# Weight column and destinations of the routed tiles: from GpSimd to VectorE

## The chip, the core and the metric

One core of a Trainium2 chip runs the kernel. The metric is the device time of one execution in microseconds. Before the change it is 798.48 us, the median of three runs (797.54, 798.48, 799.52).

## What is computed

One transformer block with adaptive layer norm on x of shape 4 x 1024 x 128: causal attention with 16 heads of 8, then a mixture of experts. Only the second half matters here:

```python
shared_out = expert(x, sg, su, sd)          # silu(x g^T) * (x u^T), times d
logits = x @ wr.T + rb                      # 7 experts
scores, idx = top_k(softmax(logits), 2)
scores = scores / scores.sum(-1)
out = shared_out
for e in range(7):
    out = out + w[..., e] * expert(x, rg[e], ru[e], rd[e])
x = x + gb * out                            # hidden width 352, model width 128
```

The kernel computes a routed expert only for the tokens that chose it.

## The kernel before

Attention fills the first 500 us or so; the change doesn't touch it. Then the 4096 tokens are normalised, the shared expert is computed in eight chunks of 512 tokens, and the router's choices are turned into slots. This is done in two groups of 2048 tokens. Each token has two choices, so a group has 4096 rows to place, and with the filling up of each expert's last tile 38 tiles of 128 rows (`STG`), 76 in all (`ST`).

A row that is scattered has 142 numbers (`RW`): 128 of the modulated token, 7 weights, one for each expert, and 7 numbers from which the destination of the result follows, one for each expert. GpSimd scatters the rows to the tensor `slot_rows_scratch` in DRAM with indirect DMAs of 128 rows (`scatter`, L782), 32 for each group. The last 24 of the second group are issued between the first routed tiles (`scatter_second`).

Each engine has its own instruction stream, and semaphores join them. The routed stage is a software pipeline written out as one function `slot_step(i, r)` for each engine. `tile(i, r, lag)` gives the tile that step r works on at that lag: tile r - lag. In step r:

- SP loads the rows of tile r+5 into `srow` (L638, four buffers). It waits until the transpose of tile t-4 (`s_rowT`) and the destinations of tile t-4 (`s_meta`) are done.
- TensorE transposes the rows of tile r+1 (L1831), multiplies tile r by gate and up (L1843), tile r-2 by down (L1854), and transposes the hidden values of tile r-1 (L1864). The transpose of tile t waits for `h_lo` of tile t-1.
- ScalarE copies the high part `h_hi` of tile r+1 (L1080), forms silu of tile r (L1087), scales the result of tile r-2 by the weight column into `y_s` (L1096, four buffers, so it waits until the scatter of tile t-4 has landed), and copies `hidT` of tile r-1 (L1103, L1105).
- VectorE forms `h_lo` of tile r+1 (L1525) and the hidden product `hid_s` of tile r (L1532). In the last twelve steps it combines the results of the first group as well (`combine`, L1510 to L1515).
- GpSimd, for tile r+2, waits for the rows, loads the tile's expert number from `expert` into a register (L831), copies that expert's weight column into `s_weight` (L832) and adds that expert's destination column to the tile's spare slots into `s_dest` (L835), a ring of twelve. Then it scatters `y_s` of tile r-3 to `routed_results_scratch` (L844), and up to step 21 it issues one scatter of the second group (L782).

`slot_steps` unrolls the steps for PE, ACT and DVE. GpSimd's and SP's middle steps are loops on the engine. The streams of VectorE and ScalarE start at step -1, that of GpSimd at step -2.

When all scatters of a group have landed, SP reads the results back (`read_results`); VectorE alone, for the second group with GpSimd (L861), adds them up and SP stores the output.

The destinations are integers held in the bits of float columns: L1388 writes them as int32, and the constant `spare` holds int32 bits (L1903).

Of the kernel before, what the change touches and what calls it, by code (L numbers as in the profile page):

```python
# [20 lines left out]
I32 = mybir.dt.int32  # L21
F32R = mybir.dt.float32r
ALU = mybir.AluOpType
# [3 lines left out]
B, S, D = 4, 1024, 128  # L27
# [4 lines left out]
T = 128  # L32
# [10 lines left out]
NE, NI = 7, 352  # L43
# [14 lines left out]
GRP = 2  # L58
# [5 lines left out]
ST = GRP * STG  # L64
RW = D + 2 * NE
SB = 4
SU = 3 * SB

CST, _at = {}, 0
# [137 lines left out]
def adaln_block(nc, x_d, wq_d, wk_d, wv_d, wo_d, sw_g_d, sw_u_d, sw_d_d, wr_d, rb_d, c_d, wmod_d,  # L207
# [10 lines left out]
    with ctx:  # L218
        def sb(name, shape, dt=F32, at=None):
            return (at or ctx).enter_context(nc.sbuf_tensor(name, shape, dt))  # L220

        def sem(name):
            return ctx.enter_context(nc.semaphore(name))
# [9 lines left out]
        cst = sb("cst", [128, CSTW])  # L233
# [68 lines left out]
        rows = sb("rows", [T, NT, RW], at=moe)  # L302
# [13 lines left out]
        tot = sb("tot", [T, GT, NE], at=moe)  # L316
# [7 lines left out]
        expert = sb("expert", [1, ST], I32, at=moe)  # L324
# [4 lines left out]
        srow = sb("srow", [T, SB, RW], at=moe)  # L329
        s_weight = sb("s_weight", [T, ST], at=moe)  # L330
        s_dest = sb("s_dest", [T, SU], I32, at=moe)
# [120 lines left out]
        s_expert = sem("s_expert")  # L452
# [3 lines left out]
        s_srow = [sem(f"s_srow{j}") for j in range(SB)]  # L456
        s_rowT = sem("s_rowT")
        s_meta = sem("s_meta")
# [10 lines left out]
        s_y_out = [sem(f"s_y_out{j}") for j in range(SB)]  # L469
# [32 lines left out]
        def slot_steps(eng, first, last, body):  # L502

            for s in range(first, last + 1):
                body(0, s)

        def tile(i, r, lag):

            t = SU * i + (r - lag)
            if isinstance(t, int) and not 0 <= t < ST:
                return None
            return t, (r - lag) % SB, SU // SB * i + (r - lag) // SB
# [5 lines left out]
        GTILES = [slice(g * GT, (g + 1) * GT) for g in range(GRP)]  # L520
# [4 lines left out]
        def needs(eng, semaphore, value):  # L525

            if not (isinstance(value, int) and value <= 0):
                eng.wait_ge(semaphore, value)
# [149 lines left out]
        def _(pool):  # L678
# [123 lines left out]
            for x in range(TOP * GT):  # L802
                k, t = divmod(x, GT)
# [16 lines left out]
            for n in range(ahead):  # L820
                scatter_second(n)

            pool.wait_ge(s_expert, GRP)

            def slot_step(i, r):
                at = tile(i, r, -2)
                if at:

                    t, j, times = at
                    pool.wait_ge(s_srow[j], 16 * times + 16)  # L830
                    e = pool.value_load(expert[0:1, bass.ds(t, 1)], min_val=0, max_val=NE - 1)  # L831
                    nc.gpsimd.tensor_copy(s_weight[:, bass.ds(t, 1)], srow[:, j, bass.ds(D + e, 1)])  # L832
                    d = (r + 2) % SU
                    needs(pool, s_y_out[j], 16 * (times - SU // SB + 1))
                    nc.gpsimd.tensor_tensor(s_dest[:, d:d + 1], srow[:, j, bass.ds(D + NE + e, 1)].bitcast(I32),  # L835
                                            cst[:, bass.ds(CST["spare"][0] + t, 1)].bitcast(I32), ALU.add).then_inc(s_meta, 1)
                at = tile(i, r, 3)
                if at:
                    t, j, times = at
                    pool.wait_ge(s_meta, t + 1)  # L840
                    pool.wait_ge(s_y, t + 1)
                    pool.sem_inc(s_seen_pool, 1)
                    d = (r - 3) % SU
                    nc.gpsimd.indirect_dma_start(y_d, bass.IndirectOffsetOnAxis(ap=s_dest[:, d:d + 1], axis=0),  # L844
                                                 y_s[:, j, :], None).then_inc(s_y_out[j], 16)
# [264 lines left out]
        def _(dve):  # L1110
            chain = [0]

            def link(ins):

                chain[0] += 1
                ins.then_inc(s_link, 1)
                dve.wait_ge(s_link, chain[0])

            V = nc.vector
# [102 lines left out]
            def ring_item(x):  # L1222

                _, kind, n, h, what = RING_PIECES[x]
                m, bank = n % 3, ring_bank(x)
                if kind in BY_ACT:
# [156 lines left out]
            def slots(g, incl):  # L1383
                before = ps[:, GROUPED, 0:GT * NE].rearrange("p (t e) -> p t e", t=GT)
                link(V.tensor_tensor(tot[:], incl, tot[:], ALU.subtract))
                link(V.tensor_tensor(tot[:], tot[:], before, ALU.add))
                link(V.tensor_tensor(tot[:], tot[:], tbase[:].unsqueeze(1).to_broadcast((T, GT, NE)), ALU.add))
                link(V.tensor_tensor(rows[:, GTILES[g], D + NE:RW].bitcast(I32), rows[:, GTILES[g], D + NE:RW], tot[:], ALU.subtract))  # L1388
                for k in range(TOP):
                    link(V.tensor_scalar(pick[:], rank[:], float(k), None, ALU.is_equal))  # L1390
                    link(V.tensor_tensor(chosen[:], pick[:], tot[:], ALU.mult))
                    link(V.reduce_sum(slot_f[:, k, :], chosen[:], AX.X))
                    V.tensor_copy(slot[:, k, GTILES[g]], slot_f[:, k, :]).then_inc(s_slot, 1)  # L1393
# [112 lines left out]
            def combine(n, part):  # L1506
                ts = chunk(n)
                if part == 0:
                    dve.wait_ge(s_y_in[n], 16 * TOP)
                    link(V.tensor_tensor(acc[:, n % 2, :, :], y_in[0][:, ts, :], y_in[1][:, ts, :], ALU.add))  # L1510
                elif part == 1:
                    link(V.tensor_tensor(acc[:, n % 2, :, :], acc[:, n % 2, :, :],
                                         gate_b[:, n * CG // TB:n * CG // TB + 1, :].to_broadcast((T, CG, D)), ALU.mult))
                else:
                    V.tensor_tensor(xs[:, ts, :], xs[:, ts, :], acc[:, n % 2, :, :], ALU.add).then_inc(s_res, 1)  # L1515
# [3 lines left out]
            def slot_step(i, r):  # L1519
                at = tile(i, r, -1)  # L1520
                if at:
                    t, j, _ = at
                    t2 = j % 2
                    dve.wait_ge(s_h_hi, t + 1)
                    V.tensor_tensor(h_lo[:, t2, :], ps[:, 0, 0:T], h_hi[:, t2, :].bitcast(F32), ALU.subtract).then_inc(s_h_lo, 1)  # L1525
                at = tile(i, r, 0)
                if at:
                    t, j, _ = at
                    t2 = j % 2
                    dve.wait_ge(s_ssilu, t + 1)  # L1530
                    needs(dve, s_shidT, t - 1)
                    V.tensor_tensor(hid_s[:, t2, :], sg[:, t2, :], ps[:, 2 + 2 * t2, 0:NI], ALU.mult).then_inc(s_shid, 1)  # L1532
                if isinstance(i, int) and first_combine <= r < first_combine + 3 * GC:
                    combine(*divmod(r - first_combine, 3))
            slot_steps(dve, -1, ST + 1, slot_step)


            for n in range(GC, NC):
# [389 lines left out]
```

## Time and profile before

| | |
|---|---|
| runs | 797.54, 798.48, 799.52 us |
| profiled execution | 797.6 us, its span 795.9 us |
| TensorE busy | 686.8 us, 86% |
| VectorE busy | 573.4 us, 72% |
| ScalarE busy | 545.9 us, 69% |
| GpSimd busy | 342.0 us, 43% |

The times of an execution count a little more than its span, which goes from the first to the last instruction. A row of a time line has the start in us from the span's start, the duration, the engine (PE is TensorE, PEld its weight load, DVE VectorE, ACT ScalarE, POOL GpSimd; a q behind it is the engine's sequencer), the line, the operation and, in brackets, how long the engine was idle before and what ended that. "issue" means that the engine waited for nothing that the profile shows. Busy time over the whole span mixes stages that have different limits, so the stretches of the routed stage are to be read one by one.

### The profile page before, as it was taken

The numbers are of one execution on the slowest core, as the hardware profiler recorded it, in microseconds if no ns is written. First come the engines' busy times: TensorE is split into PE (matmuls) and PEld (weight loads), VectorE is DVE, ScalarE is ACT, GpSimd is POOL, SyncE is SP. The second block draws the span as 40 slices with busy tenths as digits, with TensorE's granted clock in tenths as the row PEclk, the third lists the DMA queues.
The fourth block names the chain that finished last, engine by engine and source line by source line (L and its number), as shares of the span: only waits on it lengthen the run. The fifth ranks groups of instructions, "written<-read, shape, count | busy, mean of one in ns | idle before, by whom it ended". The sixth has DMA issues, their size and how long they took to land.

```text
span 795.9 us, 18082 instructions
## 1 busy us (share of the span) xinstructions
PE 686.8 (86%) x5304; PEld 395.3 (50%) x5304; DVE 573.4 (72%) x2042; ACT 545.9 (69%) x1013; POOL 342.0 (43%) x551
## 2 busy tenths in 40 slices
PE   2986899999999999999999986678869989999970
PEld 1553123333333333333333434567659889999960
DVE  5797889999999999999999834574773323333543
ACT  2785259889989888989888788544325556666640
POOL 1367613232322322232322123235657887666652
PEclk9999569999999999999999999699999999999995
DMA  9246021111111111111110079202233322223425
GB/s 260 83 156 219 1 74 47 39 30 29 47 47 48 47 28 30 41 46 47 48 37 14 1 136 178 68 23 81 63 92 78 82 76 81 66 68 104 131 87 158
DMA packets 64760, 59.46 MB, mean 75 GB/s; under 512 B 10798, under 2 KB 52398, under 8 KB 64668
## 3 DMA queue, kind: packets, MB, share of 16 engines
q1 hardware_dynamic: 58924, 46.85, 23.3%
q0 software_dynamic: 4480, 9.64, 3.4%
q10 hardware_dynamic: 1264, 1.84, 0.7%
q8 instruction: 46, 0.75, 0.4%
q14 instruction: 46, 0.38, 0.2%
HBM read 33.57 MB, written 24.33 MB: 73 GB/s over the span
## 4 chain that ended last, share of the span: by engine, by line
PE 59%; DVE 18%; ACT 9%; issue 7%; DMA 3%; POOL 1%; SPq 1%; ACTq 1%; DVEq 0%; POOLq 0%
PE ps L1658 13%; PE ps L1602 10%; PE ps L1843 9%; PE ps L1681 7%; PE ps L1854 6%; DVE junk L1238 5%; ACT probs L973 5%; PE ps L1864 3%; PE ps L1758 2%; PE ps L1636 2%; DVE junk L1210 2%; PE ps L1750 2%; DMA routed_results_scratch<-y_s,s_dest 1%; PE ps L1831 1%; DVE rot L1193 1%
## 5 line engine op out<-in xcount | busy, mean ns | idle before, releaser
L973 ACT ACTIVATE probs<-ps 128x1024 f32<-128x1024 f32 (+1 forms) x320 | 285.5, 941 | 34.5 <-PE ps L1681 32.1
L1210 DVE CUSTOM_DVE_ANT_0 junk<-ps,tri 128x512 f32<-128x512 f32 (+3 forms) x512 | 218.5, 487 | 13.9 <-PE ps L1602 11.6
L1602 PE MATMUL ps<-ka,qa 61*128 61x256 bf16 (+3 forms) x788 | 186.7, 325 | 10.0 <-DVE rowmax L1210 3.0
L775 POOL TENSOR_SCALAR_AFFINE_SELECT probs<-probs 128x512 f32<-128x512 f32 x128 | 79.7, 634 | 191.8 <-ACT probs L973 191.8
L1658 PE MATMUL ps<-probs,v 128*32 128x512 f32 (+3 forms) x1536 | 157.7, 498 | 1.3 <-POOL probs L775 1.1
L1681 PE MATMUL ps<-qa,ka 64*128 64x512 bf16 (+3 forms) x768 | 144.6, 331 | 7.7 <-ACT probs L973 5.6
L1602 PEld LDWEIGHTS ps<-ka,qa 61*128 61x128 bf16 x788 | 53.0, 95 | 159.8 <-DVE rowmax L1210 80.4
L844 POOL DMA_INDIRECT routed_results_scratch<-y_s,s_dest x76 | 76.2, 1003 | 41.0 <-issue 35.0
L782 POOL DMA_INDIRECT slot_rows_scratch<-rows,slot x64 | 64.1, 1001 | 56.6 <-DVE slot L1393 30.1
L1243 DVE TENSOR_REDUCE leftmax<-ps 128x1 f32<-128x512 f32 x120 | 78.4, 686 | 8.5 <-PE ps L1602 8.5
L1532 DVE TENSOR_TENSOR hid_s<-sg,ps 128x352 f32<-128x352 f32 x76 | 39.6, 521 | 46.2 <-ACT sg L1087 46.0
L1854 PE MATMUL ps<-wd,hidT 128*128 (+1 forms) x456 | 64.3, 277 | 5.8 <-ACT hidT L1105 5.8
L1525 DVE TENSOR_TENSOR h_lo<-ps,h_hi 128x128 fp32r<-128x128 f32 x76 | 22.2, 291 | 59.7 <-ACT h_hi L1080 59.3
L1854 PEld LDWEIGHTS ps<-wd,hidT 128*128 128x128 f32 (+1 forms) x456 | 60.6, 192 | 7.4 <-issue 7.3
L1658 PEld LDWEIGHTS ps<-probs,v 128*32 128x32 f32 x1536 | 33.8, 108 | 54.5 <-issue 49.3
L1681 PEld LDWEIGHTS ps<-qa,ka 64*128 64x128 bf16 x768 | 42.5, 94 | 33.4 <-ACT probs L973 21.2
L1087 ACT ACTIVATE sg<-ps 128x352 f32<-128x352 f32 x76 | 35.2, 463 | 33.8 <-PE ps L1843 32.0
L1096 ACT ACTIVATE y_s<-ps,s_weight 128x128 f32<-128x128 f32 x76 | 27.9, 367 | 33.5 <-PE ps L1854 25.4
L1238 DVE CUSTOM_DVE_ANT_0 junk<-ps,above 128x256 f32<-128x256 f32 x136 | 49.3, 419 | 0.0
L749 POOL TENSOR_TENSOR mrest<-mneg,mparts 32x128 f32<-32x128 f32 x16 | 6.7, 417 | 92.7 <-ACT mparts L936 92.7
L1843 PE MATMUL ps<-w_hi,h_hi 128*128 x152 | 45.3, 380 | 1.2 <-issue 1.1
L1210 DVE DVE_READ_ACCUMULATOR2_ANT rowmax<- 128x1 f32 x512 | 42.6, 83 | 0.1
(195 smaller groups left out, 1168.4 us busy)
## 6 DMA issues: line engine op xcount, KB each, us to landing
slot_rows_scratch<-cst SPq DMA_DIRECT2D x1, 5396.0 KB, 36.1
srow<-slot_rows_scratch SPq DMA_DIRECT2D x76, 71.0 KB
k_parts_scratch<-qk_parts SPq DMA_DIRECT2D x12, 320.0 KB, 2.7
ka<-k_parts_scratch SPq DMA_DIRECT2D x32, 120.0 KB
q_parts_scratch<-qk_parts SPq DMA_DIRECT2D x12, 256.0 KB, 2.6
qa<-q_parts_scratch SPq DMA_DIRECT2D x32, 96.0 KB
ka<-k_parts_scratch SPq DMA_DIRECT2D x32, 80.0 KB
xs<-in_x SPq DMA_DIRECT2D x4, 512.0 KB, 9.4
```

What stands on the lines that cost most here:

```text
L775: nc.gpsimd.affine_select(out=p, in_=p, compare_op=ALU.is_ge, fill=0.0, base=0, pattern=[[0, HQ], [1, T]], channel_multiplier=-1).then_inc ...
L782: nc.gpsimd.indirect_dma_start(slot_d, bass.IndirectOffsetOnAxis(ap=slot[:, k, t:t + 1], axis=0), rows[:, t, :], None).then_inc(s_scatter[ ...
L844: nc.gpsimd.indirect_dma_start(y_d, bass.IndirectOffsetOnAxis(ap=s_dest[:, d:d + 1], axis=0), y_s[:, j, :], None).then_inc(s_y_out[j], 16)
L973: nc.scalar.activation(probs[(n * NS + s) % 4][:, 2 * h:2 * h + 2, 0:UNTIL[s] - FROM[s]], ps[:, 2 * h:2 * h + 2, FROM[s]:UNTIL[s]], ACT.Ex ...
L1210: last = V.tensor_tensor_reduce(out=junk[:, bank - 5, at:at + w], in0=ps[:, bank, at:at + w], in1=tri[:, CH - w:CH], scale=1.0, scalar=LOW ...
L1238: last = V.tensor_tensor_reduce(out=junk[:, bank - 5, cols], in0=ps[:, bank, cols], in1=above[:, h, q - CG, :], scale=1.0, scalar=LOW, op0 ...
L1243: last = V.reduce_max(leftmax[m][:, row, q - CG:q - CG + 1], ps[:, bank, :], AX.X)
L1602: last = MM(ps[:, bank, at:at + w], qa[m][g0:g0 + KS, c0 + q * T:c0 + (q + 1) * T], ka[m][g0:g0 + KS, d0 + k0:d0 + k0 + w], start=True, st ...
L1658: last = MM(ps[VW * h:VW * (h + 1), 4, q0:CH], v4[m][:, k, h, :], probs[(n * NS + s) % 4][:, h, p0:p0 + CH - q0], start=begins, stop=ends ...
L1681: last = MM(ps[:, 2 * pair + g, at:at + CH - q0], ka[m][g * HG:(g + 1) * HG, pair * KW + kb * T:pair * KW + (kb + 1) * T], qa[m][g * HG:(g ...
L1843: last = MM(ps[:, 1 + 2 * t2 + g, 0:NI], ht[:, t2, :], wt[:, bass.ds(e, 1), g, :], start=(k == 0), stop=(k == 2))
L1854: last = MM(ps[:, 6, 0:D], hidT[0:w, t2, c, :], wd[0:w, bass.ds(e, 1), c, :], start=(c == 0), stop=(c == len(IC) - 1))
```

## The change

The two operations of L832 and L835, with their waits and the load of the expert number, go from GpSimd's `slot_step` to VectorE's. There they stand behind `hid_s` and ahead of the combining, for the same tile r+2 in step r. VectorE's steps now start at -2, behind a wait for `s_expert`. The destinations are kept as floats; the sum converts to int32 when it writes `s_dest`.

```diff
@@ GpSimd
-            pool.wait_ge(s_expert, GRP)
-
             def slot_step(i, r):
-                at = tile(i, r, -2)
-                if at:
-
-                    t, j, times = at
-                    pool.wait_ge(s_srow[j], 16 * times + 16)
-                    e = pool.value_load(expert[0:1, bass.ds(t, 1)], min_val=0, max_val=NE - 1)
-                    nc.gpsimd.tensor_copy(s_weight[:, bass.ds(t, 1)], srow[:, j, bass.ds(D + e, 1)])
-                    d = (r + 2) % SU
-                    needs(pool, s_y_out[j], 16 * (times - SU // SB + 1))
-                    nc.gpsimd.tensor_tensor(s_dest[:, d:d + 1], srow[:, j, bass.ds(D + NE + e, 1)].bitcast(I32),
-                                            cst[:, bass.ds(CST["spare"][0] + t, 1)].bitcast(I32), ALU.add).then_inc(s_meta, 1)
                 at = tile(i, r, 3)
@@ VectorE, slots()
-                link(V.tensor_tensor(rows[:, GTILES[g], D + NE:RW].bitcast(I32), rows[:, GTILES[g], D + NE:RW], tot[:], ALU.subtract))
+                link(V.tensor_tensor(rows[:, GTILES[g], D + NE:RW], rows[:, GTILES[g], D + NE:RW], tot[:], ALU.subtract))
@@ VectorE, slot_step()
                     V.tensor_tensor(hid_s[:, t2, :], sg[:, t2, :], ps[:, 2 + 2 * t2, 0:NI], ALU.mult).then_inc(s_shid, 1)
+                at = tile(i, r, -2)
+                if at:
+                    t, j, times = at
+                    dve.wait_ge(s_srow[j], 16 * times + 16)
+                    e = dve.value_load(expert[0:1, bass.ds(t, 1)], min_val=0, max_val=NE - 1)
+                    V.tensor_copy(s_weight[:, bass.ds(t, 1)], srow[:, j, bass.ds(D + e, 1)])
+                    d = (r + 2) % SU
+                    needs(dve, s_y_out[j], 16 * (times - SU // SB + 1))
+                    V.tensor_tensor(s_dest[:, d:d + 1], srow[:, j, bass.ds(D + NE + e, 1)],
+                                    cst[:, bass.ds(CST["spare"][0] + t, 1)], ALU.add).then_inc(s_meta, 1)
                 if isinstance(i, int) and first_combine <= r < first_combine + 3 * GC:
                     combine(*divmod(r - first_combine, 3))
-            slot_steps(dve, -1, ST + 1, slot_step)
+            dve.wait_ge(s_expert, GRP)
+            slot_steps(dve, -2, ST + 1, slot_step)
@@ constants
-           "spare": (np.arange(T)[:, None] + T * np.arange(ST)[None, :]).astype(np.int32).view(np.float32)}
+           "spare": np.arange(T)[:, None] + T * np.arange(ST)[None, :]}
```

## Rows read from the trace of the kernel before

**Rows 1.** Stretches: from:to, length, busy PE PEld DVE ACT POOL, clock, DMA, GB/s.
```profile
603.00:632.00 29.00, 28.93 (x218) 28.28 (x217) 11.09 (x27) 18.63 (x66) 23.01 (x40) 1.00 0.29 78
632.00:643.00 11.00, 8.34 (x48) 7.49 (x47) 2.44 (x6) 4.49 (x17) 9.15 (x16) 0.84 0.30 79
...
661.00:731.00 70.00, 70.00 (x524) 68.16 (x523) 26.53 (x65) 46.54 (x163) 45.76 (x105) 1.00 0.24 69
```
**Rows 2.** Time line of ScalarE, y_s of tiles 0, 12, 14, 21 and 23.
```profile
603.28 0.37 ACT L1096 ACTIVATE y_s<-ps,s_weight 128x128 f32<-128x128 f32 x1 [0.31 <-PE ps L1854]
...
629.05 0.37 ACT L1096 ACTIVATE y_s<-ps,s_weight 128x128 f32<-128x128 f32 x1 [0.31 <-PE ps L1854]
...
636.73 0.37 ACT L1096 ACTIVATE y_s<-ps,s_weight 128x128 f32<-128x128 f32 x1 [3.55 <-DMA routed_results_scratch<-y_s,s_dest]
...
655.37 0.37 ACT L1096 ACTIVATE y_s<-ps,s_weight 128x128 f32<-128x128 f32 x1 [2.52 <-DMA routed_results_scratch<-y_s,s_dest]
...
659.70 0.37 ACT L1096 ACTIVATE y_s<-ps,s_weight 128x128 f32<-128x128 f32 x1 [0.31 <-PE ps L1854]
```
**Rows 3.** Time line of GpSimd: first scatter of a result, one turn, scatter of tile 19.
```profile
604.45 1.00 POOL L844 DMA_INDIRECT routed_results_scratch<-y_s,s_dest  x1 [1.62 <-issue]
...
612.75 1.00 POOL L844 DMA_INDIRECT routed_results_scratch<-y_s,s_dest  x1 [0.16 <-issue]
614.06 0.97 POOL L782 DMA_INDIRECT slot_rows_scratch<-rows,slot  x1 [0.30 <-issue]
615.03 0.19 POOL L832 COPY s_weight<-srow 128x1 f32 x1
...
615.52 1.00 POOL L844 DMA_INDIRECT routed_results_scratch<-y_s,s_dest  x1 [0.16 <-issue]
...
657.04 1.00 POOL L844 DMA_INDIRECT routed_results_scratch<-y_s,s_dest  x1 [0.16 <-issue]
```
**Rows 4.** Chain of work that ended last: start us, us, what.
```profile
632.14 4.41 DMA routed_results_scratch<-y_s,s_dest
...
651.51 3.68 DMA routed_results_scratch<-y_s,s_dest
```
**Rows 5.** Time line of GpSimd, a scatter that y_s released.
```profile
708.15 1.00 POOL L844 DMA_INDIRECT routed_results_scratch<-y_s,s_dest  x1 [0.79 <-ACT y_s L1096]
```
**Rows 6.** Time line of VectorE and TensorE, a turn in the steady stretch.
```profile
712.22 0.29 DVE L1525 TENSOR_TENSOR h_lo<-ps,h_hi 128x128 fp32r<-128x128 f32 x1 [0.75 <-ACT h_hi L1080]
...
713.03 0.52 DVE L1532 TENSOR_TENSOR hid_s<-sg,ps 128x352 f32<-128x352 f32 x1 [0.51 <-ACT sg L1087]
...
713.33 0.27 PE L1831 MATMUL ps<-eye,srow 128*128 128x128 f32 x1
...
714.30 0.29 DVE L1525 TENSOR_TENSOR h_lo<-ps,h_hi 128x128 fp32r<-128x128 f32 x1 [0.75 <-ACT h_hi L1080]
```
**Rows 7.** Scatters and short VectorE operations; GpSimd's sequencer by line (ns min/median/max).
```profile
575.64 1.36 POOL L782 DMA_INDIRECT slot_rows_scratch<-rows,slot  x1 [0.56 <-DVE hid L1416]
577.32 0.96 POOL L782 DMA_INDIRECT slot_rows_scratch<-rows,slot  x1 [0.31 <-issue]
...
577.38 0.18 DVE L1359 COPY scan<-scan 128x28 f32<-128x28 f32 x1
...
579.51 0.15 DVE L1373 COPY tend<-tend 128x1 f32<-128x1 f32 x1
...
L831 POOLq FUSED_REGOPS  x112: 52/152/176, 591.9 to 760.8; - x112
L831 POOLq TENSOR_LOAD <-expert x76: 284/289/511, 591.4 to 760.5; - x76
```
**Rows 8.** Time line of VectorE, a step with combining.
```profile
755.40 0.68 DVE L1512 TENSOR_TENSOR acc<-acc,gate_b 128x512 f32<-128x512 f32 x1
756.30 0.29 DVE L1525 TENSOR_TENSOR h_lo<-ps,h_hi 128x128 fp32r<-128x128 f32 x1 [0.22 <-ACT h_hi L1080]
```
**Rows 9.** Waits of SP's queue: in total us, times, longest.
```profile
SPq L528 <- POOL s_dest L835: 63.5, 37, 4.9
```

## The prediction

> **What bounds the kernel now.** I read the busy time by stretch first, to see which engine is full where [rows 1]. The routed tiles run from about 595 to 774 us of the span, one tile a turn, 76 in all. From 661 to 731 TensorE is busy 70.00 of 70.00 us at full granted clock: its own work is the bound, and in that stretch VectorE is busy 26.53 us and GpSimd 45.76. From 603 to 632 it is the same (28.93 of 29.00). From 632 to 643 it is not: TensorE has 8.34 of 11.00 us and the granted clock has a mean of 0.84. So something else ends turns there, and the change can only pay in such a place.
>
> The time line of ScalarE says what [rows 2]. y_s of tile 0 starts at 603.28, of tile 12 at 629.05: 2.147 us a tile, TensorE's pace. Then come two long waits, 3.55 us ahead of tile 14 and 2.52 ahead of tile 21, both ended by a landing of the scatter to routed_results_scratch: y_s has four buffers, so tile t waits for the scatter of tile t-4. At TensorE's pace tile 23 would start at 603.28 + 23 x 2.147 = 652.66; it starts at 659.70. The stage has lost 7.0 us, and nothing after it gives them back, since TensorE has no idle time behind 661.
>
> Why do the scatters land late? GpSimd's time line in the early half [rows 3]: scatter of a tile at 612.75, second-group scatter at 614.06, the weight copy at 615.03, the sum behind it, next scatter of a tile at 615.52. This is 2.77 us a turn against 2.147 for TensorE. Nineteen such turns lie between the scatter of tile 0 (604.45) and that of tile 19 (657.04): 52.59 / 19 = 2.768. GpSimd falls behind by 0.62 us a turn until the four buffers are used up; from tile 13 on it sets the pace. Behind tile 19 there are no more second-group scatters and it catches up.
>
> **GpSimd's turn, after the change.** Two instructions leave it, with the load of the expert's number and its register arithmetic. From the copy's start (615.03) to the next scatter (615.52) there are 0.49 us [rows 3]. In their place comes the gap that this engine shows between one indirect DMA and the next, 0.30 us (the idle time ahead of the one at 614.06, same rows). A turn is 2.77 - 0.49 + 0.30 = 2.58 us, 0.19 less, and 19 turns give 3.6 us. The scatter of tile 19 would start at 604.45 + 19 x 2.58 = 653.5 instead of 657.04. The first one doesn't move: it waits for y_s of tile 0 anyway.
>
> How much of 3.6 reaches the end hangs on the landings. From the start of a scatter to the y_s that waits for it there were 4.59 us at tile 10 (632.14 to 636.73) and 3.86 at tile 17 (651.51 to 655.37) [rows 2, 4]; at tile 19 no more than 2.66 (657.04 to 659.70) [rows 2, 3]. If tile 17's landing is as slow again, y_s of tile 21 starts at 604.45 + 17 x 2.58 + 3.86 = 652.2, which is 3.2 us earlier; with 2.66 at tile 19, tile 23 starts at 653.5 + 2.66 = 656.1, 3.6 us earlier. I take 3.4. A landing of 4.6 at tile 19 would leave 1.6. Still GpSimd-bound in either case: tile 23 would be 3.5 us behind TensorE's pace, not 7.
>
> Upper end: the gap ahead of a scatter might be the 0.16 that stands behind the sum now [rows 3], not 0.30. Then 0.33 x 19 = 6.3 us, close to the 7.0 that are there at all. Lower end: the gap might be the lead that a scatter shows when it is released by y_s, 0.79 us [rows 5]; that is a rival below. I take 0.30 because it is the gap of a DMA behind a DMA, which the new pattern is, and in this stretch y_s has long been ready.
>
> **GpSimd elsewhere.** From 661 on its turn is already shorter than TensorE's and ends by waiting for y_s; a shorter turn gives only more waiting. Behind the last tile nothing of the changed work is left. Nothing for either.
>
> **VectorE: two instructions and a load more per tile.** Its steady turn [rows 6]: h_lo at 712.22 (0.29), hid_s at 713.03 (0.52), h_lo again at 714.30, so it works 0.81 of 2.15 us, and from hid_s's end (713.55) there are 0.75 us free. The new work stands in that gap. A 128x28 copy on this engine takes 0.18, a 128x1 copy 0.15, and I take the sum of two columns for no more [rows 7]: 0.3 to 0.36 for both. Before them the queue loads the expert's number, 0.29, and computes with it, 0.15 on GpSimd's sequencer [rows 7]; this can run under hid_s, as GpSimd's copy starts right at the end of its scatter. Lower bound 0.3, upper bound all in series 0.36 + 0.29 + 0.15 + as much again for computing the addresses = 0.95. Even then h_lo is 0.2 late, and TensorE asks for it only with the next transpose: h_lo ended at 712.51, that transpose started at 713.33, 0.82 of slack. Cost zero; VectorE could take 1.3 us a turn before it were the bound.
>
> In the last twelve steps VectorE also combines the first group: 0.68 us behind hid_s, and h_lo then follows with 0.22 idle [rows 8]. With 0.3 to 0.36 more h_lo is 0.1 late under 0.8 of slack: zero again. With the load in series too the turn would be 0.81 + 0.68 + 0.95 = 2.44, over 2.15 by 0.29, for nine steps: 2.6 us.
>
> **The waits that move with it.** VectorE now waits for the rows of tile t behind hid_s of t-2. What is queued behind that wait is h_lo of the same tile t, which needs the transpose of those very rows, and the combining, which has slack of its own; so the wait holds nothing back that TensorE asks for. The wait for the landing of tile t-12 is far from binding with four y_s buffers. The loads on SP's queue wait for the destination of tile t-4; SP stood for it 63.5 us in 37 waits [rows 9], since GpSimd ran behind. They will start earlier, and TensorE gains nothing, as it didn't wait for rows in those turns. The float form of the constants and of the 112-element subtraction costs what the integer one does.
>
> **Rivals.** (a) The port. VectorE's copy and GpSimd's descriptor writing may exclude each other. For it: a second-group scatter that ran beside VectorE's large operations took 1.36 us instead of 0.96 [rows 7]. Against it: the next one, with two short copies inside, took 0.96. If each turn's copy costs the scatter its own 0.15 to 0.19 us, the 3.6 us are eaten: 0.0 to 0.8 gained, 798 us.
> The Trainium skill (SBUF — State Buffer, "Who interferes with whom", and the warning box on SWDGE above it) has this as a rule: a float copy from SBUF to SBUF on VectorE can lock GpSimd out of the port pair and starve its descriptors; by it the sum would be about nothing. The second row speaks against it for copies as short as these.
> (b) Slower: the lead of a scatter is exposed. The sequencer of GpSimd now has only one DMA, not a copy and a sum, behind which it can prepare the next scatter with its two waits. If the 0.79 of [rows 5] shows up in each of the 19 turns, the turn is 2.58 + 0.49 = 3.07, 0.3 more than now: 5.7 us slower, 804. It decides from a gap of 0.49 up. Against: the second-group DMA behind a scatter starts after 0.30 already.
> (c) The combining steps all in series: 2.6 of the 3.4 lost, 797.7.
> (d) A larger gain, 5 to 7 us, with the gap of 0.16 or with quick landings: 792.5.
> (e) It doesn't do what it says: the landings, not GpSimd's starts, set the pace; then 0 to 1.5.
>
> **How the numbers follow.** The profiled run took 797.6 us with a span of 795.9; the median of the three is 798.5 (797.5 to 799.5). From the profiled run 797.6 - 3.4 = 794.2; from the median 798.5 - 3.4 = 795.1, which I give. What separates no change from a change here is about 0.3%, 2.4 us. Chances: forecast (gain 2.4 to 4.6) 0.56, (d) 0.08, (a), (c), (e) and slow landings, gain 0 to 2.4, together 0.23, a small loss under 2.4 from the same causes 0.03, (b) or another loss over it 0.10. Faster 0.64, same 0.26, slower 0.10. The range leaves out the far half of (d) and nearly all of (b): 792.5 to 799.
>
> **What would show it.** Right: in GpSimd's early turns a gap of 0.30 between DMAs and 2.58 a turn, the scatter of tile 19 near 653.5, less than 4 us of ScalarE's waits for landings, h_lo still followed by the transpose without a wait, same turns of 2.15 behind 661. Wrong: scatters over 1.00 us long in those turns (a), gaps of 0.5 and more (b), h_lo released by VectorE's own previous instruction and TensorE waiting for it (c). What I trust least is the length of the landings, which I can't derive.

## The result, and the profile after

Both kernels were timed twenty times on one chip. Before: median 799.16 us (797.54 to 800.44). After: 796.96 us (795.37 to 799.25). The ratio is 0.9976, interval [0.9969, 0.9983]: the change takes off 1.4 to 2.5 us. The forecast was 3.4. The profiled execution of the kernel after took 797.11 us; its span is the first line of its page. The times quoted leave out one execution of an experiment and one of the kernel before (825.81 and 917.96 us) that ran at a lower granted clock (0.817 and 0.695) throughout.

```profile
span 795.4 us, 18051 instructions
PE 689.1 (87%) x5304; PEld 395.6 (50%) x5304; DVE 595.4 (75%) x2194; ACT 546.3 (69%) x1013; POOL 313.5 (39%) x398
```

GpSimd is busy 28.5 us less and VectorE 22.0 us more; neither number says what became of the time. The stretches of [rows 1], read in the kernel after (from:to, length, busy PE PEld DVE ACT POOL, clock, DMA, GB/s), with the steps in which VectorE combines as the last row:

```profile
603.00:632.00 29.00, 29.00 (x220) 28.41 (x219) 14.86 (x54) 19.03 (x67) 20.27 (x22) 1.00 0.30 84
632.00:643.00 11.00, 10.82 (x80) 10.22 (x79) 5.33 (x21) 7.01 (x25) 8.51 (x9) 1.00 0.35 97
...
661.00:731.00 70.00, 70.00 (x523) 68.21 (x522) 35.91 (x131) 46.51 (x163) 31.54 (x33) 1.00 0.25 70
745.00:773.00 28.00, 23.91 (x167) 21.71 (x165) 16.93 (x47) 15.11 (x52) 13.41 (x13) 0.95 0.27 80
```

From 632 to 643 TensorE now works 10.82 of 11.00 us, where it had 8.34, and the granted clock is 1.00 instead of 0.84. That is the gain. The last row is where something was lost; the same stretch before:

```profile
745.00:773.00 28.00, 25.42 (x188) 24.16 (x186) 16.04 (x33) 16.95 (x60) 19.61 (x32) 1.00 0.29 88
```

TensorE had 25.42 us busy there and has 23.91, with fewer instructions in the same 28 us, since each turn is longer.

GpSimd's turn, the forecast's main term, answers to [rows 3]: the first scatter of a result, a second-group scatter, the next scatter of a result, and the one of tile 19.

```profile
605.32 0.96 POOL L831 DMA_INDIRECT routed_results_scratch<-y_s,s_dest  x1 [2.94 <-issue]
606.59 0.96 POOL L782 DMA_INDIRECT slot_rows_scratch<-rows,slot  x1 [0.30 <-issue]
607.85 0.96 POOL L831 DMA_INDIRECT routed_results_scratch<-y_s,s_dest  x1 [0.30 <-issue]
...
653.36 0.96 POOL L831 DMA_INDIRECT routed_results_scratch<-y_s,s_dest  x1 [0.31 <-issue]
```

The gap is the 0.30 that was forecast. The turn is (653.36 - 605.32) / 19 = 2.528 us, not 2.58: every scatter takes 0.96 us, where those of a result took 1.00 before.

To see what reaches the end, take as loss of a tile how far its y_s is behind TensorE's pace: (y_s of tile t) - (y_s of tile 0) - 2.1475 x t. In us, from ScalarE's time line:

```
tile                       24     60     64     73     75
before                   6.94   6.95   8.05   7.99   7.72
after                    2.41   2.46   4.17   5.89   6.19
after less before       -4.5   -4.5   -3.9   -2.1   -1.5
```

Five stages can be read from it. By tile 24, 4.5 us are won. Up to tile 60 nothing moves. From 60 to 64, where SP reads the first group's results back ahead of the rows of tile 65, both kernels lose, the one after 0.6 more. From 64 to 73, in the steps with combining, the kernel after loses 1.72 us, the one before gains 0.06: 1.8. In the last two tiles the kernel after falls back by 0.6 more, and that is the clock: the granted clock of this execution falls to 0.83 from 768 to 771 and to 0.50, the level of 1.2 GHz, behind it, with TensorE idle 0.75 us ahead of each of the last two groups of down matmuls; the last group of six then takes 1.50 us, where it took 0.93 before.

```profile
767.76 0.93 PE L1852 MATMUL ps<-wd,hidT 128*128 x6 [0.75 <-ACT hidT L1092]
768.52 0.49 PE L1862 MATMUL ps<-eye,hid_s 128*128 128x128 f32 x3
769.77 1.50 PE L1852 MATMUL ps<-wd,hidT 128*128 x6 [0.75 <-ACT hidT L1092]
```

Before, the same idle stretches stood there at full clock, and in an experiment with the same combining steps (the last one below) the clock stayed at 1.00 up to 773, and in each of the twelve experiments' traces the last two tiles lose nothing. So this 0.6 belongs to the execution.

Tile 0 starts 0.88 us later in the kernel after (604.16 against 603.28), which no median can show. In the experiments below this start lies anywhere from 602.1 to 605.7, also where nothing ahead of the stage differs. Most of the 0.88 stands there long before the changed code runs: GpSimd's last copy of `v` in the attention starts at 436.77 against 436.25, VectorE's last write of `slot` at 585.75 against 584.96. So it too belongs to the execution. What is left is 1.5 us, inside the measured interval.

Where does the turn of the combining steps get longer? VectorE in two of them, against [rows 8]:

```profile
749.99 0.28 DVE L1512 TENSOR_TENSOR h_lo<-ps,h_hi 128x128 fp32r<-128x128 f32 x1
750.40 0.52 DVE L1519 TENSOR_TENSOR hid_s<-sg,ps 128x352 f32<-128x352 f32 x1
751.14 0.15 DVE L1525 COPY s_weight<-srow 128x1 f32 x1 [0.22 <-issue]
751.28 0.16 DVE L1528 TENSOR_TENSOR s_dest<-srow,cst 128x1 int32<-128x1 f32 x1
751.36 0.68 DVE L1497 TENSOR_TENSOR acc<-y_first,y_second 128x512 f32<-128x512 f32 x1
752.08 0.29 DVE L1512 TENSOR_TENSOR h_lo<-ps,h_hi 128x128 fp32r<-128x128 f32 x1
752.97 0.52 DVE L1519 TENSOR_TENSOR hid_s<-sg,ps 128x352 f32<-128x352 f32 x1 [0.61 <-ACT sg L1074]
753.71 0.15 DVE L1525 COPY s_weight<-srow 128x1 f32 x1 [0.22 <-issue]
753.86 0.16 DVE L1528 TENSOR_TENSOR s_dest<-srow,cst 128x1 int32<-128x1 f32 x1
753.93 0.69 DVE L1499 TENSOR_TENSOR acc<-acc,gate_b 128x512 f32<-128x512 f32 x1
754.65 0.29 DVE L1512 TENSOR_TENSOR h_lo<-ps,h_hi 128x128 fp32r<-128x128 f32 x1
```

From hid_s to h_lo VectorE has no idle time but the 0.22 ahead of the copy, and h_lo no longer waits for ScalarE's h_hi (in [rows 8] it did, for 0.22). h_lo starts 0.42 us behind the end of h_hi in the mean of eight such turns (tiles 68 to 75), 0.07 before. TensorE in the first of these turns, from the chain of work that ended last (start us, us, what):

```profile
750.54 0.33 PE ps L1862 x3
750.87 0.11 PE ps L1829
750.98 0.24 issue
751.21 1.23 PE ps L1841 x6
```

Behind the transpose of the rows (L1829) TensorE stands 0.24 us with "issue", waiting for nothing that the profile names, and the gate-up (L1841) follows. h_lo ended at 750.27 (749.99 + 0.28), the gate-up started at 751.21: 0.94 us. TensorE's sequencer in that time (ns min/median/max, first and last start):

```profile
L1820 PEldq TENSOR_LOAD <-expert x1: 298/298/298, 750.4 to 750.4; - x1
L1820 PEldq FUSED_REGOPS  x1: 151/151/151, 750.8 to 750.8; - x1
L1820 PEldq SEQ_ASSERT  x1: 18/18/18, 751.0 to 751.0; - x1
```

It loads the expert's number from 750.4 on, right behind the end of h_lo, and is busy with it to 751.0. This pointed to the cause.

### The profile page after: what moved, and what is told of

Same layout as the page of the kernel before. It is cut to its first block, busy times and chain, and to the rows that moved or that the text cites. A ratio compares the mean times of both kernels' runs of the same rounds, so it can differ in the third digit from the quotient of the medians.

```text
span 795.4 us, 18051 instructions
## 1 busy us (share of the span) xinstructions
PE 689.1 (87%) x5304; PEld 395.6 (50%) x5304; DVE 595.4 (75%) x2194; ACT 546.3 (69%) x1013; POOL 313.5 (39%) x398
## 4 chain that ended last, share of the span: by engine, by line
PE 60%; DVE 17%; ACT 9%; issue 7%; DMA 3%; SPq 1%; POOL 1%; ACTq 1%; DVEq 0%; POOLq 0%
PE ps L1656 13%; PE ps L1600 10%; PE ps L1841 9%; PE ps L1679 7%; PE ps L1852 6%; DVE junk L1225 5%; ACT probs L960 5%; PE ps L1862 3%; PE ps L1756 2%; PE ps L1634 2%; DVE junk L1197 2%; PE ps L1748 2%; DMA routed_results_scratch<-y_s,s_dest 1%; PE ps L1573 1%; PE ps L1829 1%
## 5 line engine op out<-in xcount | busy, mean ns | idle before, releaser
L831 POOL DMA_INDIRECT routed_results_scratch<-y_s,s_dest x76 | 74.6, 981 | 72.5 <-DVE s_dest L1528 51.6
L1841 PE MATMUL ps<-w_hi,h_hi 128*128 x152 | 45.0, 378 | 2.0 <-issue 1.8
L1748 PE MATMUL ps<-h_hi,ws_hi 128*128 128x512 f32 (+1 forms) x48 | 22.0, 459 | 18.7 <-DVE hid L1403 18.7
```

Source lines behind the costliest of these rows:

```text
L1841: last = MM(ps[:, 1 + 2 * t2 + g, 0:NI], ht[:, t2, :], wt[:, bass.ds(e, 1), g, :], start=(k == 0), stop=(k == 2))
```

## The theory and its rival

TensorE's queue in one step is: wait for h_lo of tile t, transpose the rows of tile t+1, load the expert's number of tile t into a register, compute with it, gate-up of tile t. The load stands behind the wait. In the kernel before the least distance from the end of h_lo to the next gate-up is 0.91 us in the 32 turns of the steady stretch, and 0.96 in the mean; after, in the combining steps, 0.91 and 0.97. Only the last tile comes below (0.82 and 0.64): with no rows left to transpose, its wait for h_lo stands behind the load. A least value that recurs, whatever the stretch, looks like a floor and not like slack. Theory B: nothing of the 0.82 that I read in [rows 6] was free; an h_lo that is late makes the next gate-up late. Its rival, the prediction's own account: h_lo has slack, and the loss has another source (the read-back, landings, the port).

## The experiments

Each median stands beside that of the kernel before on the same chip. All losses are those of the table's definition.

**Combining out of the way.** In the kernel after, the twelve combining parts come behind the last routed step:

```diff
-                if isinstance(i, int) and first_combine <= r < first_combine + 3 * GC:
-                    combine(*divmod(r - first_combine, 3))
...
             slot_steps(dve, -2, ST + 1, slot_step)
+            for n in range(GC):
+                for part in range(3):
+                    combine(n, part)
```

On SP's queue the second read-back goes ahead of the first store.

> The changed kernel, but the twelve parts of combining the first group (8.3 us of VectorE) stand behind the last step, where VectorE is idle for 11.8 us, and SP reads back the second group before it stores the first. Theory A: VectorE's chain in the last steps is short again, turns of 2.15, 2.0 to 2.5 us faster than the changed kernel, less up to 1 us for four stores that now stand ahead of the last ones: 794.5 to 796. Rival (the loss isn't VectorE's): 797 or a little more.

Measured: 795.77 against 799.12, ratio 0.9961 [0.9947, 0.9975]. That is in the expected range, but only 1.2 us under the kernel after, and the two intervals overlap. The trace is clearer: the loss is 3.88 at tile 64 and 3.66 at tile 73, so these steps cost nothing. VectorE with the two new instructions but without the combining:

```profile
751.24 0.15 DVE L1525 COPY s_weight<-srow 128x1 f32 x1 [0.22 <-issue]
751.39 0.16 DVE L1528 TENSOR_TENSOR s_dest<-srow,cst 128x1 int32<-128x1 f32 x1
751.78 0.29 DVE L1512 TENSOR_TENSOR h_lo<-ps,h_hi 128x128 fp32r<-128x128 f32 x1 [0.23 <-ACT h_hi L1067]
```

h_lo waits for h_hi again. So the loss of the combining steps needs both: the new work and the combining on one engine.

**The new work back on GpSimd for the tiles whose steps combine** (67 to 75):

```diff
+                if at and isinstance(at[0], int) and at[0] >= LATE:      # LATE = 67, GpSimd's stream
...
+                    nc.gpsimd.tensor_copy(s_weight[:, bass.ds(t, 1)], srow[:, j, bass.ds(D + e, 1)])
...
-                if at:
+                if at and at[0] < LATE:                                  # VectorE's stream
```

> The changed kernel, but for tiles 67 to 75 (those whose weight and destination fall into the steps with combining) GpSimd forms them again, from floats, with one more copy to int32. Theory A: in those steps VectorE's extra 0.5 us stands in the chain hid_s, copy, sum, combining, h_lo, gate-up and stretches the turns from 2.15 to about 2.4. Then this is 2.0 to 2.5 us faster than the changed kernel (797.0), so about 794.7 or a ratio of 0.994 to 0.995 to the kernel before, and turns of 2.15 in the last ten steps. Rival: the time lost at the end comes from the loads of the rows, or what goes missing is a later start of the whole stage from run to run; then it is within 0.5 us of the changed kernel.

Measured: 796.24 against 799.12, 0.9966 [0.9957, 0.9976]. The loss from tile 64 to 73 is 0.20 us, where the kernel after has 1.72: as expected. The time is only 0.7 us better than the 796.96 of the kernel after, and the two intervals overlap; in this profile the read-back cost 3.6 us (2.47 at tile 60, 6.07 at 64). So the trace bears out where the time goes; the 2 us in the median are not shown.

**h_lo late, alone.** The kernel before, with one copy of 128x64 ahead of each h_lo:

```diff
                     dve.wait_ge(s_h_hi, t + 1)
+                    V.tensor_copy(late[:], h_hi[:, t2, 0:64].bitcast(F32))
```

> The kernel before, with one more VectorE copy of 128x128 or less (0.15 to 0.2 us) ahead of h_lo in every step, of a tile nobody reads. The prediction held that h_lo has 0.82 us of slack: then no change. Theory B: gate-up never starts less than 0.91 us behind the end of h_lo, since TensorE's sequencer waits for h_lo before it loads the expert's number (0.30 + 0.15 us) for the next products, and that floor is reached in about every second turn already; the chain spans two tiles. Then each turn gets about half of the delay longer: 0.06 to 0.1 us times 70, 4 to 7 us slower in all, turns of about 2.22 us.

Measured: 800.34 against 799.12, 1.0022 [1.0013, 1.0031]: 1.0 to 2.5 us slower. A turn of VectorE and TensorE's next gate-up:

```profile
715.39 0.19 DVE L1526 COPY late<-h_hi 128x64 f32<-128x64 f32 x1 [0.75 <-ACT h_hi L1081]
715.50 0.28 DVE L1527 TENSOR_TENSOR h_lo<-ps,h_hi 128x128 fp32r<-128x128 f32 x1
```

The copy is overlapped by the subtraction, so h_lo is late by 0.12 us, not by 0.20. The turn goes from 2.147 to 2.192 in the steady stretch, 0.045 for 0.12: some 0.07 us a turn was free, and the rest was paid. The least distance to the gate-up is 0.91 as ever. Against 0.82 of slack the result should have been none. The sign is theory B's; its 4 to 7 us were too much. They took 0.06 to 0.1 us, half of the copy's length, as paid in 70 turns. A turn of the steady stretch pays 0.045, and those that GpSimd paces pay nothing (the loss at tile 24 is 6.68, not above before's 6.94).

**TensorE's load ahead of its wait.** The decisive one, on both kernels:

```diff
             def slot_step(i, r):
+                at = tile(i, r, 0)
+                if at:
+                    expert_of(i, at[0], r)
                 at = tile(i, r, -1)
```

Nothing but the place of a register load, 0.30 us long with 0.15 of arithmetic behind it, in TensorE's stream differs. On the kernel after:

> The changed kernel with one thing moved: TensorE loads the expert's number of tile r at the head of step r, ahead of its wait for h_lo, not behind the transpose. Theory B: the 0.91 us between the end of h_lo and gate-up were that load behind that wait. Then the shortest distance falls to 0.4 to 0.6 us, the turns with combining go from 2.37 back to 2.15 or less though VectorE does what it did, the steady turns may shrink from 2.147 to 2.10, and the kernel is 2 to 4 us faster than the changed one: 793 to 795. Rival: VectorE is busy too long in those steps in itself; then the turns stay at 2.37 and the time at 797.

Measured: 790.65 against 799.03, 0.9871 [0.985, 0.9891]. VectorE and TensorE in the combining steps:

```profile
741.37 0.69 DVE L1497 TENSOR_TENSOR acc<-y_first,y_second 128x512 f32<-128x512 f32 x1
742.09 0.29 DVE L1512 TENSOR_TENSOR h_lo<-ps,h_hi 128x128 fp32r<-128x128 f32 x1
...
742.52 0.30 PE L1832 MATMUL ps<-eye,srow 128*128 128x128 f32 x1
742.65 0.58 PE L1844 MATMUL ps<-w_hi,h_hi 128*128 x2
```

From the end of h_lo (742.38) to the gate-up there are 0.27 us, and 0.43 to 0.60 in the turns of the next eight tiles. h_lo is as late as in the kernel after, 0.40 behind h_hi in the mean, and the turn (gate-up of tile 65 to that of tile 73) is 2.107 instead of 2.367; in the kernel before it is 2.16. So a late h_lo hurts by way of what TensorE's queue does between its wait and the gate-up, and by nothing else that these steps hold.

The gain is larger than the 2 to 4 us expected: 6.3 under the kernel after. Between the two traces the loss at the end differs by 5.2: 2.2 from the combining steps, 1.6 from the steady turns of tiles 24 to 60, 0.6 each from the read-back and from the clock in the last two tiles, 0.3 ahead of tile 24. Two of the five executions took 787.06 and 787.07 at a mean granted clock of 0.951, three 790.65 to 790.91 at 0.945, so the interval is wide. On the kernel before:

> The same move in the kernel before. Theory B: there the floor is only touched in every second steady turn, so at most 0.05 us a turn is gained in the 40 or so turns that GpSimd doesn't pace: 0 to 2 us faster than the kernel before. Rival: no change at all, if the floor of 0.91 is only chance.

Measured: 795.95 against 799.03, 0.9954 [0.9938, 0.997]. Its steady turn is 2.102 against 2.147, so even there the floor was part of the pace that I had called TensorE's own work. In the medians the change under study is worth more with the load moved: 795.95 - 790.65 = 5.3 us instead of 2.2.

**GpSimd's law.** The kernel before, with two more column copies on GpSimd in each tile up to step 21:

```diff
+                    if isinstance(i, int) and r <= 21:
+                        nc.gpsimd.tensor_copy(again[:, 2 * t:2 * t + 1], srow[:, j, bass.ds(D + e, 1)])
+                        nc.gpsimd.tensor_copy(again[:, 2 * t + 1:2 * t + 2], srow[:, j, bass.ds(D + e, 1)])
```

> The kernel before, with two more copies of one column per tile on GpSimd up to step 21, 0.15 to 0.19 us each, into a tile nobody reads. Theory C: GpSimd's turn sets the pace up to tile 19, and each 0.1 us more in it costs 1.9 us at the end of the stage. Then GpSimd's turn is 3.07 to 3.15 us and the kernel 5.7 to 7.2 us slower. Rival: the landings of the scatters set the pace, not their starts: 0 to 2 us slower.

Measured: 803.02 against 799.12, 1.005 [1.0035, 1.0064]: slower, but by less than the 5.7 to 7.2 expected.

```profile
611.58 0.20 POOL L833 COPY s_weight<-srow 128x1 f32 x1
611.71 0.19 POOL L835 COPY again<-srow 128x1 f32 x1
611.82 0.18 POOL L836 COPY again<-srow 128x1 f32 x1
611.97 0.18 POOL L839 TENSOR_TENSOR s_dest<-srow,cst 128x1 int32<-128x1 int32 x1
```

A copy of 0.18 to 0.20 us follows the one ahead of it after 0.11 to 0.13, so two add 0.21 to the turn (2.979 against 2.768), not 0.30 to 0.38. 19 x 0.21 = 4.0; the loss at tile 24 is 3.8 larger than before's, the time 3.9. What GpSimd's turn loses in the early half arrives nearly one for one.

**Fewer second-group scatters per turn.** GpSimd issues two in each of its first two steps, then one in three of four steps, so that its turn in the early half falls to TensorE's. On the kernel after and on the one before:

```diff
-            for s in range(-2, 2 * SU):
+            for s in range(-2, 3 * SU):
                 slot_step(0, s)
-                if ahead + s + 2 < TOP * GT:
-                    scatter_second(ahead + s + 2)
+                for _ in range(2 if s in (-2, -1) else s < 3 or s % 4 != 3):
+                    if n < TOP * GT:
+                        scatter_second(n)
+                        n += 1
...
```

> The changed kernel, with the 24 second-group scatters ordered otherwise on GpSimd: two in each of the first two steps, then one in three of four steps, up to step 25. Theory C (GpSimd's mean turn sets the pace): the mean turn falls from 2.53 to 2.21, the slip of 2.5 us that is left falls to 0.3 to 1, and the kernel is 1.5 to 2.2 us faster than the changed one: 795. Rival: the late landings of single scatters make the slip, then no more than 0.5 us.

> The same order in the kernel before. Its turn is 2.77 with and 1.50 without a second-group scatter, a mean of 2.45, so the slip of 7 us falls to 2 to 3: 4 to 5 us faster than the kernel before, 794 to 795, with VectorE left alone. If theory C is wrong: under 1.5 us.

Both missed: 800.15 against 799.03, 1.0016 [1.0002, 1.003], and 802.42, 1.0043 [1.0029, 1.0057]. GpSimd's turn did fall (2.235 and 2.435) and the loss at tile 24 with it (-0.2 and 2.5), but by tile 60 it is 4.2 and 10.4. SP's queue shows why (in total us, times, longest):

```profile
SPq L649 <- DMA slot_rows_scratch<-rows,slot: 9.3, 1, 9.3
```

SP waits for all second-group scatters ahead of the load of tile 29, though tile 38 is the first that reads their rows. With the scatters stretched out, that wait holds back the rows of nine tiles: the loss goes from -0.2 at tile 24 to 4.1 at tile 29.

**Everything that was found, together.** The load moved on TensorE, the scatters stretched out in two of three steps, and SP's wait moved to the load of tile 38; on the kernel after, on the same with the combining behind the steps, and on the kernel before. Of the edit only SP's part is shown:

```diff
-            sp.wait_ge(s_scatter[1], 16 * TOP * GT)
-            with sp.Fori(second, stop) as i:
+            for s in range(second * SU, (second + 1) * SU):
+                if s == STG - SB - 1:
+                    sp.wait_ge(s_scatter[1], 16 * TOP * GT)
+                load_rows(0, s)
+            with sp.Fori(second + 1, stop) as i:
```

> The changed kernel with TensorE's early load and with the second-group scatters spread (two in each of the first two steps, then two in three steps, up to step 28), and SP's wait for them moved from the load of tile 29 to that of tile 38, which is the first to need them. Theory D: the earlier spreading took away the slip of 2.5 us up to tile 24 and then lost 4.3 at one wait of SP that stands too early. Then the slip up to tile 40 is under 0.5 us, and the kernel 2 us or more faster than with the early load alone (790.65): 787 to 789. Rival: the rows of the second group are really needed earlier, or the scatters disturb the loads: 791 or more.

> The same with the combining moved behind the last step and the second group read back before the first is stored. With the early load the combining steps take 2.107 us a turn already, so 0 to 0.5 us more is to be had: 786.5 to 789.

> The early load and the spread scatters in the kernel before, whose weights and destinations are GpSimd's. Its mean turn is 2.77 x 2/3 + 1.50 / 3 = 2.35 against 2.09 for TensorE over 25 turns, so a slip of 6.4 less the 5 or so that the buffers take: 1 to 2 us slower than the same on the changed kernel. If it is equal, the change under study is worth nothing once the two other brakes are off.

Measured: 787.06 (0.9856 [0.984, 0.9873]), 787.21 (0.9859 [0.984, 0.9878]) and 792.0 (0.9925 [0.9908, 0.9942]), against 799.12. The first is 12 us below the kernel before and the best version here. GpSimd's turn in it is 2.128 us, no more than 0.02 over TensorE's 2.108 (tiles 0 to 24), and TensorE never stops in the half where both kernels lost their time:

```profile
603.00:661.00 58.00, 58.00 (x443) 57.56 (x442) 30.60 (x110) 39.13 (x137) 43.99 (x46) 1.00 0.31 91
```

Taking the combining out brings nothing more, as it should once a late h_lo is harmless. The change under study is worth 792.0 - 787.06 = 4.9 us in this surrounding, against an expected 1 to 2: without it GpSimd's turn is 2.369, still over TensorE's new 2.1, and the loss at tile 24 is 2.9 instead of none.

**VectorE's load ahead of its wait.** The kernel after, with `value_load` at the head of VectorE's step.

> The changed kernel, with VectorE's load of the expert's number moved to the head of the step, ahead of h_lo. It tells how much of the cost in the combining steps is that load (0.30 + 0.19 us on the sequencer, 0.21 us of idle time behind hid_s in the trace) and how much the two operations. Theory A: of the 0.52 us that the chain got longer about 0.2 go; the turns with combining fall from 2.37 to about 2.27, 0.8 us faster than the changed kernel. Rival: the load ahead of h_lo delays h_lo itself, and the turns get longer everywhere.

Measured: 796.41 against 799.12, 0.9969 [0.9957, 0.9981]; not to be told from the kernel after. The idle 0.22 ahead of the copy did go:

```profile
751.29 0.52 DVE L1522 TENSOR_TENSOR hid_s<-sg,ps 128x352 f32<-128x352 f32 x1 [0.63 <-ACT sg L1074]
751.73 0.15 DVE L1528 COPY s_weight<-srow 128x1 f32 x1
751.79 0.15 DVE L1531 TENSOR_TENSOR s_dest<-srow,cst 128x1 int32<-128x1 f32 x1
751.86 0.69 DVE L1497 TENSOR_TENSOR acc<-y_first,y_second 128x512 f32<-128x512 f32 x1
753.21 0.29 DVE L1515 TENSOR_TENSOR h_lo<-ps,h_hi 128x128 fp32r<-128x128 f32 x1 [0.67 <-DVE acc L1497]
```

but here h_lo stands idle for 0.67 us, and the turn is 2.41, not the 2.27 expected. VectorE's sequencer has the reason:

```profile
L1509 DVEq TENSOR_LOAD <-expert x1: 305/305/305, 752.6 to 752.6; - x1
L1509 DVEq FUSED_REGOPS  x1: 190/190/190, 752.9 to 752.9; - x1
```

The load starts when the combining part has ended (751.86 + 0.69 = 752.55), and h_lo waits behind it in the queue. In the turn ahead of this one it started at 749.4, beside hid_s, and h_lo followed without idle time. The kernel says why that is one turn of three: the first two of the three combining parts go through `link`, which puts a semaphore wait for their end behind them in VectorE's queue, and the third doesn't. In all six turns behind a first or second part the load starts 0.04 us behind the part's end; in both turns behind a third it starts under hid_s. So this load was moved ahead of one wait and stayed behind another. That reading is argued from the trace; no run leaves these waits out.

## Why the prediction was right or wrong

- **What bounds the kernel** (right). GpSimd paces tiles 13 to 19, and its turn acts nearly one for one: the longer turn of 2.979 and the shorter of 2.528 both came out in the loss at tile 24.
- **GpSimd's turn** (right mechanism, undersized). 0.49 out, 0.30 in, as forecast. In addition each scatter of a result went from 1.00 to 0.96, so a turn gave 0.24, not 0.19: 19 x 0.24 = 4.6 where 3.6 stood. Of it 4.5 arrived by tile 24, since y_s now waits less for landings; I had taken 3.4. The waits of y_s, in us in total, times, longest (7.5, 4 and 3.5 before):

```profile
ACT y_s L1083 <- DMA routed_results_scratch<-y_s,s_dest: 4.9, 4, 2.0
```

- **The port**, rival (a) (wrong). The scatters beside VectorE's copy and sum take 0.96 us, less than before. The Trainium skill (SBUF — State Buffer, "Who interferes with whom") names both kinds of operation, a copy and a sum with both inputs in SBUF, among those that can contend with GpSimd; for operations of 0.15 us, the scatters' 0.96 shows nothing of it. Beside the combining's operations of 0.69 us the scatters do take longer, 1.05 to 1.40 us, where GpSimd has idle time to spare.
- **The exposed lead**, rival (b) (wrong). The gap is 0.30 in these turns.
- **VectorE's cost in the steady stretch** (right). The turn is 2.147 before and after; h_lo waits for h_hi with 0.23 idle.
- **VectorE's cost in the combining steps** (the step that failed). The prediction says that h_lo is "0.1 late under 0.8 of slack: zero again". It is 0.35 later than before (0.42 against 0.07), and the slack was about 0.07, as the run with a late h_lo shows. The steps cost 1.8 us where the sum had nothing. Two errors lie in it. The first and larger: the slack was read from h_lo's end to the transpose, in a turn where TensorE's array was busy with other work until then ([rows 6]). What waits for h_lo is TensorE's queue, which afterwards still transposes, loads a number and computes with it; from h_lo to gate-up there are never less than 0.91 us in a turn that has a transpose. The engine's rows say "busy", and hide that the sequencer is just as full. The second: VectorE's own load is hidden under hid_s only in part (it starts with it, at 750.4 and 753.0), and 0.22 idle us stand ahead of the copy, in a turn where the combining takes all that is left. By the rows above, from gate-up (751.21) to hid_s 1.76, to the copy 0.74, to the combining 0.22, to h_lo 0.72, to the next gate-up but one (755.86) 1.21: 4.65 us for two tiles, against 4.29 at 2.147.
- **Rival (c)** was nearly this: 2.6 us over nine steps against the 1.8 that were lost. Its condition, all in series, stood among causes worth 0.23 together. It priced the engine's turn and not TensorE's floor, but its place was the right one; what failed was its chance.
- **The read-back** was not in the prediction at all. The rows of tile 65 come behind it in SP's queue, and the step at tiles 60 to 64 is 1.1 before, 1.7 after, and between 0.5 and 3.6 in the other profiles. It varies by execution, but the change has a part in it. The prediction says of SP's loads that they "will start earlier, and TensorE gains nothing". They do for tiles 12 to 32, and from tile 33 on they start later: SP's load waits for the destination of tile t-4, which GpSimd in the steady stretch had ready 1.8 us ahead of that tile's transpose; VectorE, behind hid_s, has it 0.74 us behind the transpose's start. SP stood 111.6 us in 65 waits for it, against 63.5 in 37 [rows 9]. The buffers hide this for the loads, and the read-back, next in the queue, is late by it. The transpose of tile 60 and the first DMA of the read-back, before and then after:

```profile
730.57 0.27 PE L1831 MATMUL ps<-eye,srow 128*128 128x128 f32 x1
731.70 0.39 SPq L661 DMA_DIRECT2D y_first<-routed_results_scratch  x1
...
726.93 0.27 PE L1829 MATMUL ps<-eye,srow 128*128 128x128 f32 x1
728.58 0.39 SPq L661 DMA_DIRECT2D y_first<-routed_results_scratch  x1
```

  This distance is 1.13 us in all six traces in which GpSimd forms the destination, and 1.64 or 1.65 in seven of the eight in which VectorE does; it is 1.26 in the eighth, where VectorE's load stands at the head of its step. The step at tiles 60 to 64 is larger with the change in each of four pairs of kernels that differ by nothing else, by 0.3 to 0.8. So the 0.6 is mostly the change's; no run tests it alone.

The sum in the end: -4.5 (early turns) + 0.6 (read-back) + 1.8 (combining) + 0.6 (clock of that execution) = -1.5 in the profiles, and -2.2 in the medians. The forecast had -3.4 for the first term and zero for the others. So it erred by 1.1 too little gained and by 2.4 not foreseen, and these partly cancel: that the median came within 1.2 us of the forecast is in part luck.

## What to carry to other kernels

Slack is the distance from a result to the work that needs it, less everything that the waiting queue still does behind the wait: read it on the sequencer, as the least distance over many turns, and take an unvarying least distance for a floor. Put register loads ahead of a queue's wait, where they run while the engine is busy. When work leaves an overloaded engine, look up in every stage what the receiving engine does there, the rare stage above all, and which queues wait for the result that now comes at another point of the step.

## What the runs showed of the hardware

- A register load with its arithmetic behind a semaphore wait sets a floor of 0.91 us from the end of VectorE's write to TensorE's matmul, the transpose between them included; with the load ahead of the wait the least distance is 0.27. TensorE shows it as "issue" or not at all. The load itself, of one number from SBUF, takes 0.298 us in the row above. The Trainium skill (DMA: Bandwidth & Descriptors, "Latency and other measured facts") gives `tensor_load` a floor of some 600 ns and doesn't say from which memory; for this load the rows don't bear it out.
- An indirect DMA of 128 rows takes 0.96 us of GpSimd behind another DMA and 1.00 behind its own copy and sum; beside VectorE's combining it takes 1.05 to 1.40.
- Small instructions in a row overlap: one more copy of 0.19 us on GpSimd adds 0.105 to its turn, one of 0.20 us on VectorE makes what follows 0.12 late.
